# Neighbour sums with the node places as the stationary operand, products in two fp32r parts, and two of four relations blocks read by TensorE

## The reference

```python
h = layernorm(x)
m = clifford_linear(h[src] * r[edge_type], msg_w, msg_b)         # 256 -> 256
m = m * sigmoid(r[edge_type] @ gate_w.T + gate_b)
m = m * max(deg_src[src] * deg_dst[dst], 1) ** -0.5
x = x + clifford_linear(h + segment_sum(m, dst), upd_w, upd_b)
z = layernorm(x)
w = softmax(mean(z[None], 0) @ Wr + br)                          # 8 weights for each node
for e in range(8):                                               # 256 -> 256 -> 256 -> 256
    y[e] = relu(bn(relu(bn(z @ W1[e] + b1[e])) @ W2[e] + b2[e])) @ Wo[e] + bo[e]
out = x + sum(w[:, e] * y[e] for e in range(8))
```

## Time and profile before

| | us |
|---|---|
| median of 3 runs | 1954.49 (1953.44 to 1954.67) |
| profiled execution, its own time | 1955.06 |
| its span | 1953.0 |
| TensorE busy, 13045 matmul records | 1869.2 |
| POOL busy | 1399.4 |
| ScalarE busy | 1005.7 |
| VectorE busy | 787.6 |
| mean granted TensorE clock | 0.981 |

### The profile page before, as it was taken

The page is one execution under the profiler, slowest core; times in us unless marked ns, Lnnn a source line. Parts: engine busy times, 40 slices in busy tenths (PEclk is TensorE's granted clock), DMA queues, the critical chain, the costliest instruction groups (busy, mean ns, idle before and its releaser), DMA issues.

```text
span 1953.0 us, 35233 instructions
## 1 busy us (share of the span) xinstructions
PE 1869.2 (96%) x13045; PEld 1690.8 (87%) x13046; DVE 787.6 (40%) x1834; ACT 1005.7 (51%) x2286; POOL 1399.4 (72%) x1410
## 2 busy tenths in 40 slices
PE   6848988999999999999999999999999999999998
PEld 6837887988998998998998998998998998998888
DVE  8953332333333334343343343333333343333342
ACT  6444644545555555555555555554554554553445
POOL 4877777777777777777777777777777777777600
PEclk9968989999999999999999999999999999999999
DMA  8185444434434434444444443443443443444400
GB/s 244 52 292 176 125 114 117 125 106 127 121 103 127 123 103 125 125 108 121 125 113 116 126 123 105 126 123 103 126 124 104 125 125 103 125 112 108 93 12 6
DMA packets 91761, 232.32 MB, mean 119 GB/s; under 512 B 24748, under 2 KB 39210, under 8 KB 91679
## 3 DMA queue, kind: packets, MB, share of 16 engines
q0 software_dynamic: 66336, 184.06, 35.5%
q1 hardware_dynamic: 24528, 46.21, 7.2%
q10 hardware_dynamic: 815, 1.16, 0.2%
HBM read 217.90 MB, written 13.44 MB: 118 GB/s over the span
## 4 chain that ended last, share of the span: by engine, by line
PE 87%; POOL 5%; DVE 3%; issue 3%; DMA 1%; ACT 1%; DVEq 0%; POOLq 0%; SPq 0%
PE z L755 34%; PE y L785 17%; PE agg L800 17%; PE pr L809 9%; POOL H L405 3%; PE y L731 3%; PE y L722 2%; POOL R L405 2%; DVE H L939 2%; PE y L677 2%; PE z L707 1%; PE y L743 1%; PE y L723 1%; PE y L777 1%; ACT big L508 1%
## 5 line engine op out<-in xcount | busy, mean ns | idle before, releaser
L405 POOL DMA_INDIRECT H<-h_table,src x784 | 770.8, 983 | 238.9 <-issue 236.5
L405 POOL DMA_INDIRECT R<-r_table,typ x598 | 615.3, 1029 | 199.2 <-issue 197.9
L593 ACT ACTIVATE h<-z,bns 128x256 f32<-128x256 f32 (+1 forms) x864 | 417.3, 539 | 627.1 <-PE z L755 624.6
L1144 DVE SCALAR_TENSOR_TENSOR acc<-y,wg,acc 128x256 f32<-128x256 f32 x392 | 173.4, 479 | 699.8 <-PE y L785 699.7
L800 PE MATMUL agg<-S,H 128*86 128x64 f32 x4704 | 398.5, 242 | 0.7 <-issue 0.7
L800 PEld LDWEIGHTS agg<-S,H 128*86 128x86 f32 x4704 | 394.5, 160 | 2.0 <-issue 1.2
L755 PE MATMUL z<-hT,big 128*128 128x256 f32 (+1 forms) x1728 | 385.2, 366 | 1.9 <-ACT h L593 1.9
L785 PE MATMUL y<-big,h 128*128 128x256 f32 x1568 | 378.2, 382 | 1.7 <-DVE lg L1107 1.6
L755 PE MATMUL z<-h,big 128*128 128x256 f32 (+1 forms) x1728 | 375.5, 360 | 0.4
L755 PEld LDWEIGHTS z<-h,big 128*128 128x128 f32 x1728 | 304.9, 190 | 36.8 <-ACT h L593 1.0
L785 PEld LDWEIGHTS y<-big,h 128*128 128x128 f32 x1568 | 291.3, 190 | 42.1 <-issue 1.9
(11 more groups left out here) (162 smaller groups left out, 1070.7 us busy)
## 6 DMA issues: line engine op xcount, KB each, us to landing
H<-h_table,src POOLq DMA_INDIRECT x784, 2.8
tb<-in_typ_row SPq DMA_DIRECT2D x24, 448.0 KB
R<-r_table,typ POOLq DMA_INDIRECT x598, 2.8
h_table<-big SPq DMA_DIRECT2D x7, 910.0 KB, 8.8
big<-in_x SPq DMA_DIRECT2D x7, 896.0 KB, 10.9
big<-in_w SPq DMA_DIRECT2D x8, 768.0 KB, 4.8
acc<-in_x SPq DMA_DIRECT2D x22, 256.0 KB, 5.4
out<-acc SPq DMA_DIRECT2D x22, 256.0 KB
```

The costliest lines, as they stand in the source:

```text
L405: pool.indirect_dma_start(out=to[:, b * DX:(b + 1) * DX], out_offset=None, in_=tab, in_offset=bass.IndirectOffsetOnAxis(ap=ix[:, J * SB + ...
L593: last = s_.activation(o[:, m, 0:wide_], z_[:, m, 0:wide_], ACT.Relu, bias=bns[:, l, 1, c:c + 1], scale=bns[:, l, 0, c:c + 1])
L1144: last = v.scalar_tensor_tensor(out=acc[:, g % 3, t, :], in0=b[:, t * D:(t + 1) * D], scalar=wg[:, t, e_:e_ + 1], in1=acc[:, g % 3, t, :], ...
```

## The change

- **Sums.** The places (node mod 128) are the stationary operand now, S of 128 x 128 for each block in fp32r, and the products move, 258 columns. Since fp32r keeps fewer bits, a product is split: ScalarE rounds it to HI (`high_act`), VectorE makes LO = H - HI (`low_dve`), and TensorE multiplies both: 4 blocks x 2 parts = 8 fp32r matmuls for each superblock. Two superblocks share a PSUM bank O; nodes are on partitions.
- **Masked adds.** Place modulo 128 leaves the tile open. VectorE adds a bank to one or two tiles of `sums` in SBUF, multiplied by a mask for each tile (`take_dve`). AGG, the carry, the zeroing and the column register go.
- **x2.** Sums have nodes on partitions now, so TensorE transposes them (`at_pe`, at s4), ScalarE copies them (`at_act`) and `x2_pe` follows at s5 with two matmuls for each tile instead of three. The bias is added by VectorE (mbias, gs).
- **Relations.** TensorE reads two blocks of four (`read_blocks`), POOL gathers two. `types_act` builds two one-hot sets, PR has two banks. A read of superblock j waits for the product of superblock j - 1 (`prod`).
- **Rings.** NH 8 to 6, R 45 blocks to 32, 2 for each superblock (16 superblocks instead of 15). POOL waits for `lo_ready` instead of `mm`. END becomes 6, 10, 18, ..., 186, 190, 194, 196.
- **Start.** The flags are computed in another way (distances within a pair of superblocks), masks are made, and the experts' biases are prepared after the first products.

The core of the diff:

```diff
-NH = 8
-RB = 45
-GB = 3
-TC = 8
+NH = 6
+RB = 32
+NR = 16
+TC = 16
+NA = 4
+def read_blocks(j, whole):
+    return [] if j >= whole else [(2 * j + i, SB - 2 + i) for i in range(2)]
...
-        S = sb("S", [P, 2, SB, W])
+        S = sb("S", [P, 2, SB, P], f32r)
+        HI = sb("HI", [P, 2, SB * DX], f32r)
+        LO = sb("LO", [P, 2, SB * DX], f32r)
+        sums = sb("sums", [P, NA, D + 2])
+        masks = sb("masks", [P, NM, NPR])
...
-                        pool.wait_ge(mm, J - NH + 1)
+                        pool.wait_ge(lo_ready, J - NH + 1)
                         gather_h(J)
...
+                def high_act(J):
+                    if J >= NSB:
+                        return
+                    act.wait_ge(prod, J + 1)
+                    if J > 1:
+                        act.wait_ge(mm, J - 1)
+                    s_.activation(HI[:, J % 2, :], H[:, J % NH, :], ACT.Copy).then_inc(hi_ready, 1)
...
+                    def at_act(g):
+                        t0, nt = GROUPS[g]
+                        for t in range(nt):
+                            z_ = full()
+                            copy(aT[:, t, :, :], z_[:, :, 0:P]).then_inc(z_free, 1)
...
-                    def ffn(g, hook):
+                    def ffn(g, hook, between):
                         for s in range(NE + 2):
                             if s < NE:
                                 layer(0, s, h1[:, s % 2, :, :], wide[g])
+                            between()
                             if 0 < s <= NE:
                                 layer(1, s - 1, h2[:, (s - 1) % 2, :, :], wide[g])
                             hook(f"s{s}")
...
+                    def sb_act(some, later):
+                        for J in some:
+                            rest()
+                            types_act(J + 3)
+                            waiting.append(J + 2)
+                        if not later:
+                            rest()
+
+                    def rest():
+                        while waiting:
+                            high_act(waiting.pop(0))
...
-                def sb_pe(J, j):
-                    col = pe.value_load(base_i[0:1, ds(J, 1)], min_val=0, max_val=512 - W)
-                    pe.wait_ge(prod, J + 1)
-                    if not isinstance(J, int) or J + 1 < WHOLE:
-                        rel_pe(J + 1, j + 1)
+                def sb_pe(i, j):
+                    if not isinstance(i, int) or j + 2 < WHOLE:
+                        rel_pe(i, j + 2)
+                    pe.wait_ge(lo_ready, i * (2 * STEP) + (j + 1))
+                    if j % 2 == 0 and j > 2:
+                        pe.wait_ge(o_free, i * STEP + (j // 2 - 1))
                     for b in range(SB):
-                        for m in range(3):
-                            last = pe.matmul(AGG[0:M3, m, ds(col, W)], H[:, j % NH, b * DX + m * M3:b * DX + (m + 1) * M3],
-                                             S[:, j % 2, b, :], start=False, stop=True, skip_group_check=True)
+                        for x in (HI, LO):
+                            last = pe.matmul(O[:, j // 2 % 2, 0:D + 2], S[:, j % 2, b, :], x[:, j % 2, b * DX:b * DX + D + 2],
+                                             start=j % 2 == b == 0 and x is HI, stop=j % 2 == 1 and b == SB - 1 and x is LO)
                     last.then_inc(mm, 1)
...
+                    for q, b in read_blocks(j, max(WHOLE, j + 1)):
+                        pe.wait_ge(oh_t, i * (4 * STEP) + (q + 1))
+                        if j:
+                            pe.wait_ge(prod, i * (2 * STEP) + j)
...
+                def take_dve(upto):
+                    for j in range(taken[0], upto // 2):
+                        dve.wait_ge(mm, 2 * j + 2)
...
+                def prod_dve(J):
+                    dve.wait_ge(gr[J % NR], gathered(J))
+                    dve.wait_ge(gh[J % NH], 64 * (J // NH + 1))
+                    cut = PLACE[J][1] * DX
+                    last = v.tensor_tensor(H[:, J % NH, 0:cut], H[:, J % NH, 0:cut], rows(J), ALU.mult)
+                    for q, b in read_blocks(J, WHOLE):
+                        dve.wait_ge(rel_full, q + 1)
+                        h_ = H[:, J % NH, b * DX:b * DX + D + 2]
+                        last = v.tensor_tensor(h_, h_, PR[:, q % 2, 0:D + 2], ALU.mult)
+                    last.then_inc(prod, 1)
...
+                def sb_dve(some):
+                    for J in some:
+                        take_dve(J)
+                        low_dve(J + 1)
+                        prod_dve(J + 2)
```

More of the change, by code:

```diff
@@ L37, in sizes, with edges @@
         t += w
[L38 to L44, removed]
+    def edges(t, sign):
+        p = min(1.0, t * P / n)
+        return e * p + sign * 5.5 * sqrt(e * p * (1 - p))
+    done = [min(nsb, 2 * ceil(edges(t + 1, 1) / (2 * SE))) for t in range(nt)]
+    needed = [done[t0 + w - 1] for t0, w in groups]
+    twos = [g for g, (t0, w) in enumerate(groups) if w == 2]
+    step = max(2, round(P * e / (n * SE)) * 2)
+    lead = max([needed[g] - step * (groups[g][0] + 2) // 2 for g in twos] + [2])
     ends = []
@@ L47, in sizes @@
         end = step * (t0 + 2) // 2 + lead if w == 2 else needed[g]
-        ends.append(min(nsb, max([end, 1] + ends[-1:])))
+        ends.append(min(nsb, max([end, 2] + ends[-1:])))
     ends[-1] = nsb
+    tiles = []
+    for j in range(nsb // 2):
+        lo = min(sum(done[t] <= 2 * j for t in range(nt)), nt - 1)
+        hi = max([t for t in range(nt) if edges(t, -1) < (2 * j + 2) * SE] + [lo])
+        tiles.append((lo, hi))
     assert n < nt * P
-    whole = ends[pairs[-1]] if pairs else nsb
-    alike = [g for g in pairs if g + 2 in pairs and ends[g + 1] - ends[g] == step == ends[g + 2] - ends[g + 1]]
+    whole = ends[twos[-1]] if twos else nsb
+    alike = [g for g in twos if g + 2 in twos and ends[g + 1] - ends[g] == step == ends[g + 2] - ends[g + 1]]
     loop = range(alike[0], alike[-1] + 1) if alike else range(0)
-    return nt, nsb, groups, ends, step, loop, whole
+    loop = loop[:len(loop) // 2 * 2]
+    return nt, nsb, groups, ends, step, loop, whole, tiles
+def read_blocks(j, whole):
+    return [] if j >= whole else [(2 * j + i, SB - 2 + i) for i in range(2)]
 def ring(nsb, whole):
@@ L154, in build @@
         dd = sb("dd", [P, 2])
+        gs = sb("gs", [P, 2])
         st = sb("st", [P, 2, 6])
@@ L680, in _ @@
                 pe.wait_ge(cl_ready, 1 + 2 * len(NEG))
-                for m in range(3):
+                for k in range(2):
+                    pe.matmul(PR[:, 0, 0:D], mbb[:, k, :], UT[:, k, :], start=k == 0, stop=k == 1)
+                for m in range(2):
                     for k in range(2):
-                        last = pe.matmul(AGG[0:M3, m, 0:D], km[:, k, m * M3:(m + 1) * M3], UT[:, k, :],
+                        last = pe.matmul(O[:, m, 0:D], km[:, k, m * P:(m + 1) * P], UT[:, k, :],
                                          start=k == 0, stop=k == 1)
@@ L1010, in _ @@
+                link(v.scalar_tensor_tensor(out=c_hi, in0=d_max, scalar=float(1 - P), in1=c_hi, op0=ALU.add, op1=ALU.max))
+                for k in range(NM):
+                    v.tensor_scalar(masks[:, k, :], d_to, float(k * P), None, ALU.is_equal)
+                link(v.tensor_tensor(c_hi, c_hi, c_lo, ALU.max))
+                link(v.reduce_max(flag[:, 0:1], c_hi, AX.X))
+                v.scalar_tensor_tensor(out=flag[:, 0:1], in0=flag[:, 1:2], scalar=-1.0, in1=flag[:, 0:1],
                                        op0=ALU.mult, op1=ALU.max).then_inc(flag_in, 1)
@@ L1089, in x2_dve @@
                         dve.wait_ge(y_free, no + YS)
+                        for t in range(nt):
+                            x_ = acc[:, g % 3, t, :]
+                            last = v.scalar_tensor_tensor(out=x_, in0=mbias[:, :], scalar=gs[:, t:t + 1], in1=x_,
+                                                          op0=ALU.mult, op1=ALU.add)
+                        link(last)
                         for t in range(nt):
```

476 lines of the change are left out of this document (264 added, 212 removed).

## The result

The changed kernel takes **2045.92 us** (median of 4 runs, 2041.48 to 2052.65), the kernel before 1953.97 (4 runs, 1952.48 to 1954.67): ratio 1.0475, 95% interval 1.0445 to 1.0504. The forecast was 2002 with a range of 1950 to 2045: right that it gets slower, wrong by 44 us in size, and just outside the range.

What follows compares the result with a forecast made beforehand. TensorE and POOL were taken as equally long in steady groups, POOL as the early bound. Span 1953.0 - 2 (ramp) + 16 (sums, reads) - 11 (end) + 44 (ScalarE stalls) = 2000, so about 2002 us; range 1950 to 2045.

Steps and rivals of the forecast that it cites:

- Step 1: TensorE's sums: eight fp32r matmuls take 0.97 us per superblock instead of 24 records, saving 0.87 us.
- rival E: TensorE's sums miss the fp32r rate, 0.22 instead of 0.121 us per matmul: +157 us, 2159 us, chance 0.03.
- Step 2: TensorE reads two relations blocks instead of one: eight more matmuls, +0.97 us per superblock.
- Step 3: TensorE's x2 update: 0.43 us less work per group, against a 0.45 us stall behind the transposes; net 0.
- Step 4: POOL: 48 gathers instead of 56 per group at 1.29 us, 62 of 72 us, so it gets slack.
- Rival C: POOL's relief reaches TensorE through a ramp faster by 24 us, with small group stalls: 1936 us, chance 0.12.
- Step 5: VectorE's added work per group: 27.2 us becomes about 44 of 72, covered, so no cost.
- Step 6: ScalarE's in-order work fits at 58.7 of 72 us but stalls TensorE 2.2 us per group: +44 us in all.
- Rival B: ScalarE's outputs come in time, stalls are covered and TensorE's sum alone stands: 1958 us, chance 0.17.
- D: ScalarE's HI waits behind VectorE's product, one microsecond more at two places per group: 2042 us, chance 0.13.
- Step 7: The ramp to the third group: first sum about 145, first layer 188, third group 299; gain 2 us.
- The last superblocks: TensorE's last 12 superblocks have no reads, so cheaper sums save 11 us there.

Runs made afterwards that it cites:

- e1: Changed kernel with TensorE's groups written out instead of a loop of ten times two groups: 2019.26 us.
- e4: Changed kernel with TensorE's groups written out and two ScalarE steps (copy hxT, next group's norm) moved earlier: 1985.77 us.
- e6: As e4, but TensorE reads two relations blocks in even superblocks and one in odd ones: 1950.77 us.
- e5: As e4, but TensorE reads one relations block per superblock, so POOL makes 56 gathers per group: 2062.16 us.
- e8: As e4, but two reads in three of eight superblocks, otherwise one, each waiting only for its PSUM bank's last product: 1964.50 us.

## Why the prediction was wrong in size, step by step

- **Missed: the loop.** This is the step that failed: a term put at nothing without a reason. The part-by-part list names every engine's work, but not TensorE's program itself. The diff has `loop = loop[:len(loop) // 2 * 2]`, and the loop's body went from one group to two. I gave it no cost and no rival. It is worth 30 of the 44 us (e1), and with it the forecast would have been 2032, within my range.
- **Step 1, sums: right.** From 912.74 to 913.57 seven of them start, 0.119 us each, eight in 0.95 us; rival E is out. The section of the Trainium skill that I cited there (TensorE: Matmul & The Clock Gate, Back-to-back issue gap) gives its formula for an isolated matmul, and for a stream of loads and matmuls 81 ns each at 128 columns and 131 ns at 512; the stream is this kernel's case, and 119 ns at 258 columns lies between the two.
- **Step 2, reads: right.** 0.95 us per read (e4 against e6).
- **Step 3 and the sum of 1 to 3: nearly.** The stall behind the transposes is 0.26 us and not 0.45. TensorE's work is +0.78 us per group (72.86 against 72.08) where the steps together gave +0.37 (0.80 - 0.43); with the stall 1.04 for 0.82, 4 us over 20 groups. I did not trace those 0.4 us of work.
- **Step 4, POOL: right for this kernel, wrong in its price.** POOL waits for the low part (248.7 us from 380 to 1900 us, the line below), so it does have slack. But its gathers do not keep their 1.29 us when VectorE does more. Here this is hidden; e5 to e8 show what it costs where it is not. Rival C rested on POOL's relief and did not come.

```profile
L440 POOL DMA_INDIRECT H<-h_table,src x637 | 665.2, 1044 | 424.5 <-DVE LO L1304 248.7 <-issue 175.8
```

- **Step 5, VectorE: right in the sum** (42 against 44 us), **and not quite covered**: 0.6 us per group at the first read, for the product of the superblock before. I had named this wait as the price if the cover were gone, and put it at nothing.
- **Step 6, ScalarE's order: right in kind, and in the sum by luck.** Predicted 2.2 us per group. The order is worth 1.5 us per group ((1506.8 - 1476.2) / 20, e1 to e4): the wait from s0 to s1 is 0.5 us and not 1.2, s1 to s2 0.8 for 1.0. With the wait for the product (step 5), which was not in this step, it is 2.1. Rival B (covered) is out. D's time, 2042 us, is near the measured one, but its mechanism is not there: HI waits for products 17.6 us in the whole kernel, under 1 us per group, and D asked for over 2.

```profile
L583 ACT ACTIVATE HI<-H 128x1040 fp32r<-128x1040 f32 x196 | 209.1, 1067 | 25.4 <-DVE H L1291 17.6
```

- **Step 7, the ramp: nearly.** First sum at 147.71 (145 predicted), first layer at 192.96 (188), third group's first layer at 300.57 (299). The fourth transformation comes 1.8 us later than before; I had 2 earlier.

```profile
147.71 0.42 PE L873 MATMUL o<-HI,S 128*128 128x258 f32 x1 [1.01 <-DVE LO L1304]
...
192.96 1.95 PE L825 MATMUL z<-hT,big 128*128 128x128 f32 x16
...
300.57 1.89 PE L825 MATMUL z<-hT,big 128*128 128x256 f32 x8
```

- **The last superblocks** gave 6 us and not 11.

The sum, term by term, over the forecast's span of 2000: ramp 1.8 for -2 (+4), end -6 for -11 (+5), loop +30, and the 20 groups without the loop 65 for 60 (+5): 44 us. Only the loop is a mechanism that I did not have.

## What to carry to other kernels

List the program of each engine among the things that a diff changes: where a loop's body grows, count its returns and give the return a price; written out straight, the same code cost nothing here. When work is moved onto an idle engine, ask in what order it stands there and not only whether it fits: 1.5 us per group came back by moving two calls. And a time per instruction read from a trace holds for the neighbours that it had: a gather took 1.29 us beside 27 us of VectorE work per group and 1.36 to 1.375 (e5, e6, e8) beside 42.

## What the runs showed that I had not expected

- A return of TensorE's loop with two groups in the body stands still for 2.0 to 3.1 us and, with the lower clock behind some of them, costs 3.3 us in the changed kernel and 5.3 in the kernel before; with one group in the body there is no such row.
- With TensorE's code in straight order, 1.72 MB of instructions are brought instead of 0.43, with no effect on the time (1954.06 against 1953.91 us).
- An added VectorE instruction of 0.72 us per superblock with one SBUF input costs the kernel before 42 us, one of 1.24 us with two inputs 24 us, with VectorE busy for 33 to 37 of 73 us in a group. About 15 of the 24 us are VectorE's own product coming late; in the kernel with one input VectorE waits 305.5 us for gathered rows.
- In the changed kernel written out, TensorE and POOL are so evenly loaded that the splits between reads and gathers that I tried (56, 53, 52 and 48 gathers per group) ended at groups of about 76, 72, 71 and 73.8 us; the kernel before has 72.1.
